# Last expert layer of a 1-core megakernel: half of the routed tiles turned by DMA, POOL's work in two parts per group, late gathers in the weights' place

## Chip, cores and metric

One core of one Trainium2 chip. The metric is the device time of one launch in microseconds. Before the change three runs gave 1920.95, 1926.91 and 1927.06 us; the median is 1926.91 us.

## What is computed

Two layers, each a residual attention and a residual expert feed-forward, on 16 sequences of 256 tokens with 256 features:

```python
x = x + tanh(g_xattn[0]) * xattn0(layernorm(x), ctx)
x = x + tanh(g_ffn[0])   * moe0(layernorm(x))
x = x + tanh(g_xattn[1]) * xattn1(layernorm(x), ctx)
x = x + tanh(g_ffn[1])   * moe1(layernorm(x))      # the part that is changed

def moe1(x):                    # 4096 tokens, 16 experts of width 128, 4 per token
    tidx, tw = route(x)         # sigmoid scores, best 2 of 4 groups, best 4 experts
    h  = silu(x @ gate_w[e].T) * (x @ up_w[e].T)          # per chosen expert
    routed = sum_k tw[k] * (h @ down_w[e_k].T)
    shared = (silu(x @ sh_gate.T) * (x @ sh_up.T)) @ sh_down.T   # width 256
    return routed + shared
```

## The kernel before

The kernel is written as hand-ordered streams, one per engine, in blocks that end with a barrier. Fp32 values are carried as two fp16 halves, upper and lower, so that a product is three matmuls.

The last layer (`moe1`) takes the tokens in four blocks of 1024. Each token row (two halves, 512 fp16) is **scattered** by POOL with indirect DMAs into a DRAM table `routed` of its block, ordered by expert. A table has 48 tiles of 128 rows, taken as 12 **groups** of 4 tiles, so there are 48 groups (r = 0 to 47). For a group, SP loads its 4 tiles into one of three buffers in `r_space` (L764, 512 KB). PE turns them, two tiles at a time (8 transposes into one PSUM bank, `turn_rows`, L1984), and ACT copies each half out to `m_rowsT` (`take_rows`, L2162, 128x1024). PE then makes the hidden layer (`routed_hidden`, L2040, 12 matmuls a half), ACT and DVE make silu, the product (L2169, L2266) and its two halves (L2176, L2272), PE turns these (`turn`, L2053), DVE copies them out (L2278), PE makes the down product (`routed_down`, L2014), ACT copies that to `m_y` (`evict`, L2188) and SP stores it to DRAM (L1875, 512 KB). POOL **gathers** the four expert rows of each token back (L1918) and DVE adds them with their weights to `x_res` (`combine`, L2287, 8 instructions for a pair of token tiles). Eight **shared jobs** of 512 tokens go through the shared expert, two ahead of the groups and six behind (L1999, L2014, L2297).

What one step r of the loop over groups does:

- PE: turn half 0 of group r+1, hidden half 0 of r, down of r-2, turn half 1 of r+1, hidden half 1 of r, load the experts' numbers of r+1 into registers, turn the hidden layer of r-1.
- ACT: silu(r-1), take half 0 of r+1, upper half of the hidden layer, take half 1 of r+1, evict(r-2). A take waits for the hidden matmuls two places back, since `m_rowsT` has two buffers; evict(r) waits for the store of r-3, since `m_y` has three.
- DVE: hiddenT copy (r-2), product and lower half (r-1), in some steps a piece of the routing of a later block, and `combine` of a pair in the steps of `PAIR_AT` (20, then every second step from 30 to 48).
- SP: load(r) once the buffer's rows have been turned, then store(r-6).
- POOL: behind the hidden matmuls of r-1, four scatters or gathers (`PACED`, `PER_GROUP = 4`). A gather waits for `used`: it has four token tiles of buffer (`GB = 4`).

The last pairs of token tiles (11 to 15) are combined among the shared jobs behind the groups, by `COMBINE_BEHIND`; SP's `finish(b)` stores block b of the output, 1 MB each.

## Time and profile before

| | |
|---|---|
| median of three runs | 1926.91 us (1920.95 to 1927.06) |
| profiled execution | 1910.97 us, its span 1908.7 us |
| granted TensorE clock, mean | 0.945 |
| PE busy | 1651.9 us, 87% |
| DVE / ACT / POOL busy | 62% / 53% / 40% |
| DMA | 256.99 MB, 135 GB/s over the span |

Columns of a window row: stretch, length, then busy time with instruction counts for each engine, the granted clock of TensorE (1.0 is full speed), the share of time that a DMA engine was busy, and GB/s. In a timeline row the first number is the start in us from the span's start, the second the length, and the bracket gives the idle time before it and what ended it. "Remote" or "unknown" there means that the profile has no releaser. The last layer runs from about 1450 us to the end.

### The profile page before, as it was taken

The page shows a single profiled execution, that of the slowest core. Times are in us where ns is not written, and L with a number is a line of the kernel's source. Part 1 is how long each engine was busy: PE and PEld are TensorE (multiplying, and loading weights), DVE is VectorE, ACT ScalarE, POOL GpSimd, SP SyncE. Part 2 cuts the span into 40 slices and gives each one's busy share as a digit, 9 for nine tenths or more (in the row PEclk, how much of TensorE's full clock was granted, in tenths as well). Part 3 has the DMA queues.
Part 4 walks back from the last instruction along what each step waited for, and adds up shares of the span by engine and source line. Part 5 has one row for each costly group of instructions (what it writes and reads, how often), then busy time and mean ns, then how long its engine had stood idle before and what let it go on. Part 6 is the DMA issues. An engine that isn't in the chain of part 4 may idle for free. (4 is left out here: it accounts for less than half of the span.)

```text
span 1908.7 us, 44330 instructions
## 1 busy us (share of the span) xinstructions
PE 1651.9 (87%) x16920; PEld 1256.1 (66%) x16920; DVE 1188.1 (62%) x2667; ACT 1005.9 (53%) x1744; POOL 763.4 (40%) x932
## 2 busy tenths in 40 slices
PE   4699999758999999999995899999886898888885
PEld 3355666437888888888883566665643777776753
DVE  4678887735555565565566788777762556345546
ACT  4377877635445444444433456645544576555541
POOL 2155657875310101000036334423651535565534
PEclk9699999978999999999997999989997999999898
DMA  9753333214645544544224434423243456677523
GB/s 288 208 117 68 72 60 68 57 41 133 203 150 196 172 139 167 195 158 135 67 84 107 99 80 79 71 55 58 76 125 144 164 200 233 232 235 250 190 90 121
DMA packets 297700, 256.99 MB, mean 135 GB/s; under 512 B 198047, under 2 KB 270155, under 8 KB 296216
## 3 DMA queue, kind: packets, MB, share of 16 engines
q1 hardware_dynamic: 271256, 168.84, 32.5%
q0 software_dynamic: 26240, 85.32, 13.4%
q8 instruction: 141, 2.31, 0.5%
q14 instruction: 63, 0.52, 0.1%
HBM read 102.98 MB, written 107.74 MB: 110 GB/s over the span
## 5 line engine op out<-in xcount | busy, mean ns | idle before, releaser
L1643 PE MATMUL ps<-m_xT,m_w_halves 128*128 128x256 f16 x3360 | 413.9, 273 | 2.2 <-issue 2.2
L1643 PEld LDWEIGHTS ps<-m_xT,m_w_halves 128*128 128x128 f16 x3360 | 329.4, 98 | 41.4 <-issue 2.8
L1158 ACT ACTIVATE a_probs<-ps 128x1024 f32<-128x1024 f32 (+1 forms) x256 | 234.8, 917 | 183.8 <-PE ps L995 181.9
L1662 PE MATMUL ps<-m_w_halves,m_hiddenT 128*128 128x256 f16 x1680 | 229.8, 273 | 5.1 <-DVE m_hiddenT L1758 4.6
L1274 POOL TENSOR_TENSOR a_probs<-a_probs,a_half_above 128x512 f32<-128x512 f32 x128 | 162.3, 1270 | 157.2 <-ACT a_probs L1158 156.6
L1719 ACT ACTIVATE m_hiddenT<-m_hidden 128x256 f16<-128x256 f32 x280 | 116.6, 416 | 197.6 <-DVE m_hidden L1755 191.6
L1758 DVE TENSOR_TENSOR m_hiddenT<-m_hidden,m_hiddenT 128x256 f16<-128x256 f32 x280 | 119.2, 426 | 135.1 <-ACT m_hiddenT L1719 130.7
L1610 POOL DMA_DIRECT2D expert_out<-m_y x40 | 28.9, 722 | 434.8 <-DVE m_y L1738 432.2
L2162 ACT ACTIVATE m_rowsT<-ps 128x1024 f16<-128x1024 f16 x112 | 115.9, 1035 | 154.0 <-remote 93.8
L1357 DVE TENSOR_REDUCE a_qT<-ps 128x4 f16<-128x1024 f32 x128 | 156.5, 1223 | 51.1 <-PE ps L1006 50.2
L1662 PEld LDWEIGHTS ps<-m_w_halves,m_hiddenT 128*128 128x128 f16 x1680 | 163.5, 98 | 26.9 <-DVE m_hiddenT L1758 7.2
L995 PE MATMUL ps<-a_Q,a_K 32*128 32x256 f16 (+1 forms) x2048 | 145.6, 261 | 34.2 <-DVE a_qT L1357 25.0
L1918 POOL DMA_INDIRECT m_gathered<-routed_out,r_routed_row x128 | 127.6, 997 | 113.4 <-DVE x_res L2287 46.6
L1755 DVE TENSOR_TENSOR m_hidden<-ps,m_silu 128x256 f32<-128x256 f32 x280 | 117.9, 421 | 81.9 <-ACT m_silu L1715 77.9
L1715 ACT ACTIVATE m_silu<-ps 128x256 f32<-128x256 f32 x280 | 105.6, 377 | 102.3 <-PE ps L1643 99.1
L1354 DVE TENSOR_REDUCE a_block_max<-ps 128x6 f32<-128x768 f32 x128 | 121.7, 951 | 60.4 <-PE ps L1006 58.8
L995 PEld LDWEIGHTS ps<-a_Q,a_K 32*128 32x128 f16 x2048 | 81.8, 93 | 114.2 <-issue 80.4
L2040 PE MATMUL ps<-m_w_halves,m_rowsT 128*128 x1152 | 149.0, 279 | 2.7 <-issue 2.6
L748 POOL DMA_INDIRECT routed<-r_halves,r_routed_row x96 | 96.6, 1007 | 132.1 <-issue 38.3
L1026 PE MATMUL ps<-a_probs,a_v_ext 128*32 128x256 f32 (+1 forms) x2048 | 126.6, 366 | 1.8 <-POOL a_probs L1274 1.8
L2040 PEld LDWEIGHTS ps<-m_w_halves,m_rowsT 128*128 128x128 f16 x1152 | 108.0, 100 | 21.7 <-issue 5.6
L1006 PE MATMUL ps<-a_K,a_Q 32*128 32x256 f16 (+1 forms) x1024 | 96.3, 267 | 10.3 <-DMA a_K<-a_kT 5.5
(319 smaller groups left out, 3070.3 us busy)
## 6 DMA issues: line engine op xcount, KB each, us to landing
routed<-m_zeros POOLq DMA_DIRECT2D x32, 768.0 KB
r_space<-routed SPq DMA_DIRECT2D x48, 512.0 KB
routed_out<-m_y SPq DMA_DIRECT2D x48, 512.0 KB
r_w_load<-in_L_w SPq DMA_DIRECT2D x24, 896.0 KB
dispatched<-r_xT SPq DMA_DIRECT2D x10, 1024.0 KB, 6.6
expert_out<-m_y POOLq DMA_DIRECT2D x40, 256.0 KB
a_ctx_in<-in_ctx SPq DMA_DIRECT2D x32, 256.0 KB
m_experts_load<-in_L_experts SPq DMA_DIRECT2D x18, 384.0 KB, 3.5
```

The source lines that it names most:

```text
L995: last = mm(SC[:, b_, c0:c0 + S - q0], lhs[r, g, kt * P:(kt + 1) * P], rhs[r, g, q0:S], start=not second and not causal_band, stop=second ...
L1026: last = mm(psum[j * SLOT:(j + 1) * SLOT, 6, (g % 2) * S + q0:(g % 2 + 1) * S], v[:, i % 4, kt, g * GH + j, :], pr[:, g % 2, j, kt * S:(kt ...
L1158: A(pr[:, g % 2, 2 * jp:2 * jp + 2, :], SC[:, :, 0:SPAN], ACT.Exp, scale=1.0 / math.sqrt(DH)).then_inc(asem["ex"], 1)
L1274: pool.tensor_tensor(two, two, half[:, :].unsqueeze(1).unsqueeze(1).broadcast_to([P, 2, 2, P]), ALU.mult).then_inc(asem["mask"], 1)
L1354: last = V.tensor_reduce(bmax[:, h0:h0 + 2, :], MX[:, :, 0:SPAN].rearrange("p h (b k) -> p h b k", k=P), AX.X, ALU.max, negate=True)
L1357: last = V.tensor_reduce(qT2[:, m % 3, :, h0:h0 + 2, DH].rearrange("p t h -> p h t"), MX.rearrange("p h (t k) -> p h t k", t=TT), AX.X, AL ...
L1643: last = mm(psum[:, v % HB, m * CH:(m + 1) * CH], wh[:, u, ws_, m, d_ * F0 + f_ * P:d_ * F0 + (f_ + 1) * P], xT[:, q % XB, xs_ * KT + d_, ...
L1662: last = mm(psum[:, 4 + 2 * (q % 2) + t, 0:D], hT[:, hs_, f_, t * P:(t + 1) * P], wh[:, u, ws_, 2, f_ * D:(f_ + 1) * D], start=f_ == 0 and ...
L1755: V.tensor_tensor(hp[:, v % 2, :], psum[:, v % HB, CH:2 * CH], hsb[:, v % 2, :], ALU.mult)\
L1758: V.tensor_tensor(hT[:, 1, v % FT, :], hp[:, v % 2, :], hT[:, 0, v % FT, :], ALU.subtract)\
L1918: pool.indirect_dma_start(yb[:, nt % GB, k, :], None, eo[b], bass.IndirectOffsetOnAxis(ap=rows[:, nt, k:k + 1], axis=0)).then_inc(got[nt % ...
L2040: last = mm(psum[:, 2 * (q % 2) + half, t % 2 * 2 * P:(t % 2 + 1) * 2 * P], xd[:, l % 2, xs_ * KT + d_, t * P:(t + 1) * P], both, start=k ...
```

## The change

- The first two tiles of each group are no longer loaded and turned by PE. `turn_routed_rows` brings them by two transposing DMAs from `routed` straight into the turned layout, in `r_space`, whose three places now hold turned rows (they take the part of `m_rowsT`, also for the shared jobs). The last two tiles are loaded into a new buffer `m_routed_rows` and turned by PE and taken by ACT as before. So `turn_rows(.., 0)` and `take_rows(.., 0)` do nothing for a routed group.
- SP issues, for group r: the load of two tiles; then, behind a wait for the hidden matmuls of group r-3, the two transposing DMAs; then store(r-6).
- PE's turn of half 1 waits for all three transfers of its group.
- POOL's four scatters or gathers of a step are split: two behind the hidden matmuls, two behind the first half of the down matmuls of r-2.
- The gathers of the last block (token tiles 24 to 31) go into the place of the routed experts' weights. Those of tiles 28 to 31 have semaphores of their own and wait for no `combine`.
- `COMBINE_BEHIND` takes pairs 11 to 15 behind jobs 1 to 5, so pair 15 is combined ahead of the last job's add. The last block's output is stored in three parts (512, 256 and 256 KB).

ACT's stream in a step of the groups' loop, before (names as in the profile; the brackets are semaphores waited for; `m1_rows_turned` is PE's turn, `f_h_done` the hidden matmuls):

```order
L2169 ACTIVATE m_silu<-ps 128x512 [waits f_gated,f_h_done]
L2162 ACTIVATE m_rowsT<-ps 128x4x256 [waits f_h_done,m1_rows_turned]
L2176 ACTIVATE m_hidden_halves<-m_hidden 128x512 [waits m1_hidden_turned,f_gated]
L2162 ACTIVATE m_rowsT<-ps 128x4x256 [waits f_h_done,m1_rows_turned]
L2188 ACTIVATE m_y<-ps 128x512 [waits m1_y_sent1,m1_y_done]
L2188 ACTIVATE m_y<-ps 128x512 [waits m1_y_done]
```

and with the change:

```order
L2214 ACTIVATE m_silu<-ps 128x512 [waits f_gated,f_h_done]
L2221 ACTIVATE m_hidden_halves<-m_hidden 128x512 [waits m1_hidden_turned,f_gated]
L2207 ACTIVATE r_space<-ps 128x4x256 [waits f_h_done,m1_rows_turned]
L2233 ACTIVATE m_y<-ps 128x512 [waits m1_y_sent1,m1_y_done]
L2233 ACTIVATE m_y<-ps 128x512 [waits m1_y_done]
```

The take of half 0 is gone, and the one that is left stands behind the upper half.

SP's stream about the store of the first output block, before (`m1_y_out` is ACT's evict, `m1_combined` DVE's combine):

```order
L764 DMA r_space<-routed 128x4x512 [waits m1_rows_turned]
L1875 DMA routed_out<-m_y 128x4x256 [waits m1_y_out]
L1881 DMA out_x<-x_res 128x8x256 [waits m1_y_out,m1_combined]
L764 DMA r_space<-routed 128x4x512 [waits m1_rows_turned]
L1875 DMA routed_out<-m_y 128x4x256 [waits m1_y_out]
```

and with the change:

```order
L1902 DMA routed_out<-m_y 128x4x256 [waits m1_y_out]
L1908 DMA out_x<-x_res 128x8x256 [waits m1_y_out,m1_combined]
L1892 DMA m_routed_rows<-routed 128x2x512 [waits m1_rows_turned]
L765 DMA_TRANSPOSE r_space<-routed 128x4x128 [waits f_h_done]
L765 DMA_TRANSPOSE r_space<-routed 128x4x128
L1902 DMA routed_out<-m_y 128x4x256 [waits m1_y_out]
```

A store now stands behind a wait for hidden matmuls and two transposing DMAs.

The diff, cut to its core:

```diff
@@ helpers
+    def turned_rows(place):
+        return r1["space"][:, place % XB1 * ROWS_T:(place % XB1 + 1) * ROWS_T].rearrange("p (a n) -> p a n", a=2 * KT)
...
+    def turn_routed_rows(sp, place, r):
+        for t in range(2):
+            r0 = (r % GROUPS1 * QT + t) * P
+            sp.dma_start_transpose(turned_rows(place)[:, :, t * P:(t + 1) * P], routed[r // GROUPS1][r0:r0 + P, :])\
+              .then_inc(x_in[r % XB1], 16)
@@ end of attention(1), sync
-                    for r in range(XB1):
-                        load_routed_rows(sp, r)
+                    turn_routed_rows(sp, 2, 0)
@@ moe1
-        xd = sb("rowsT", [P, 2, 2 * KT, CH], F16)
+        xr = sb("routed_rows", [P, XB, 2, 2 * D], F16)
+        late_rows = wh.rearrange("p s e n -> p (s e n)")[:, 0:RT * K1 * D * 2].bitcast(F32)\
+            .rearrange("p (t k d) -> p t k d", t=RT, k=K1)
+        LATE = (RG - 1) * RT
+        def rows_gathered(nt):
+            if nt >= LATE + GB:
+                return got_late[nt - LATE - GB], 16 * K1
+            return got[nt % GB], GOT0 + 16 * K1 * (nt // GB + 1)
-        COMBINE_BEHIND = {1: 11, 3: 12, 4: 13, 5: 14}
+        COMBINE_BEHIND = {1: 11, 2: 12, 3: 13, 4: 14, 5: 15}
+        def turned_until(l):
+            return l + min(l, L0) + max(l - L1, 0)
@@ moe1, sync
                 def load(r):
-                    sp.wait_ge(xp_done, 2 * (L0 + r - XB + 1))
+                    l = L0 + r
+                    if r >= XB:
+                        sp.wait_ge(xp_done, turned_until(l - XB) + 1)
...
+                    r0 = (r % GROUPS * QT + 2) * P
+                    sp.dma_start(xr[:, r % XB, :, :], ...).then_inc(x_in[r % XB], 16)
+                    if r:
+                        sp.wait_ge(h_done, H0 + last_unit(l - XB) + 1)
+                        turn_routed_rows(sp, l, r)
...
-                for b in range(1, RG):
+                for b in range(1, RG - 1):
                     finish(b)
+                for pairs, job, half in ((2, 6, 1), (4, 7, 0), (4, 7, 1)):
+                    sp.wait_ge(used, RT * K1 * (RG - 1) + 2 * K1 * pairs)
+                    sp.wait_ge(y_out, 2 * place_of_job(job) + half + 1)
...
@@ moe1, gpsimd
-                        if nt >= GB and k == 0:
+                        if GB <= nt < LATE + GB and k == 0:
                             pool.wait_ge(used, 2 * K1 * ((nt - GB) // 2 + 1))
...
                 for r in range(NR):
                     pool.wait_ge(h_done, H0 + U0 + r)
+                    paced(r, 0)
+                    if r >= 2:
+                        pool.wait_ge(y_done, 2 * (L0 + r - 2) + 1)
+                    else:
+                        pool.wait_ge(xp_done, 2 * (L0 + r + 2))
+                    paced(r, 1)
@@ moe1, tensor: turn_rows, routed_hidden
                         if half == 0:
-                            pe.wait_ge(x_in[r % XB], X0[r % XB] + 16 * (r // XB + 1))
-                        tile = [rows_of(r)[:, t, :] for t in range(QT)]
+                            return
+                        pe.wait_ge(x_in[r % XB], X0[r % XB] + 48 * (r // XB + 1))
+                        tile = [None, None] + [xr[:, r % XB, t, :] for t in range(2)]
...
-                    pe.wait_ge(xp_out, 2 * l + half + 1)
                     if half == 0:
+                        pe.wait_ge(x_in[r % XB], X0[r % XB] + 48 * (r // XB + 1))
                         pe.wait_ge(g_done, H0 + q - 1)
+                    else:
+                        pe.wait_ge(xp_out, turned_until(l + 1))
@@ moe1, scalar: take_rows
-                    if l >= L1 + JB:
+                    routed_place = L0 <= l < L1
+                    if l >= L1 + JB or routed_place and half == 0:
                         return
...
-                    if l >= 2:
-                        act.wait_ge(h_done, H0 + last_unit(l - 2) + 1)
+                    if l >= XB:
+                        act.wait_ge(h_done, H0 + last_unit(l - XB) + 1)
@@ moe1, vector, end
                 add_job(JA + JB - 1)
-                combine(15)
```

## Rows read from the trace of the kernel before

**Rows 1.** Windows: groups r = 0 to 8, 8 to 31 and 31 to 47.

```profile
1493.53:1551.28 57.75, 51.77 (x537) 45.34 (x537) 31.97 (x91) 38.17 (x60) 22.52 (x22) 0.94 0.55 186
1551.28:1707.30 156.02, 133.31 (x1439) 113.78 (x1436) 73.61 (x157) 96.32 (x146) 91.48 (x92) 1.00 0.70 233
1707.30:1825.05 117.75, 94.94 (x930) 77.98 (x928) 59.04 (x110) 62.98 (x96) 63.89 (x65) 0.93 0.65 209
```

**Rows 2.** Chain of waits, 1676 to 1690 us: start us, us, what.

```profile
1681.73 1.03 ACT m_rowsT L2162
...
1682.90 0.61 PE ps L1984 x8
...
1686.13 1.84 PE ps L1984 x8
...
1687.99 1.03 ACT m_rowsT L2162
```

**Rows 3.** Timeline, PE, the same group.

```profile
1683.35 1.47 PE L2040 MATMUL ps<-m_w_halves,m_rowsT 128*128 x12
...
1684.66 1.47 PE L2014 MATMUL ps<-m_w_halves,m_hiddenT 128*128 x12
...
1685.97 0.61 PE L1984 MATMUL ps<-ident,r_space 128*128 128x128 f16 x8
...
1686.41 1.47 PE L2040 MATMUL ps<-m_w_halves,m_rowsT 128*128 x12
...
1687.72 0.61 PE L2053 MATMUL ps<-ident,m_hidden_halves 128*128 128x128 f16 x8
```

**Rows 4.** Timeline, ACT, DVE and POOL, the same group.

```profile
1677.09 0.94 POOL L1918 DMA_INDIRECT m_gathered<-routed_out,r_routed_row  x1 [0.30 <-issue]
...
1682.65 1.08 ACT L2188 ACTIVATE m_y<-ps 128x512 f32<-128x512 f32 x2
...
1683.61 0.62 ACT L2169 ACTIVATE m_silu<-ps 128x512 f32<-128x512 f32 x1
...
1684.99 0.66 ACT L2176 ACTIVATE m_hidden_halves<-m_hidden 128x512 f16<-128x512 f32 x1
...
1685.68 0.69 DVE L2272 TENSOR_TENSOR m_hidden_halves<-m_hidden,m_hidden_halves 128x512 f16<-128x512 f32 x1 [0.74 <-issue]
```

**Rows 5.** Groups of instructions, 1551.28 to 1707.30 us: busy us, mean ns | idle before.

```profile
L2162 ACT ACTIVATE m_rowsT<-ps 128x1024 f16<-128x1024 f16 x46 | 47.8, 1039 | 51.6 <-remote 34.1 <-PE ps L1984 17.4
```

**Rows 6.** DMA queues, 1551.28 to 1707.30 us: packets, MB, share of 16 engines.

```profile
q1 hardware_dynamic: 24288, 24.12, 46.3%
q0 software_dynamic: 4365, 11.93, 22.9%
```

**Rows 7.** Timeline: SP in the first expert layer.

```profile
738.11 2.52 SPq L1560 DMA_TRANSPOSE m_xT<-dispatched  x2
```

**Rows 8.** DMA queues, 738 to 742 us: mean share in tenths, 40 slices of 0.1 us.

```profile
DMA  9779196990000037999741000001489996300006
```

**Rows 9.** DMA in the last attention, 1140 to 1240 us.

```profile
DMA packets 19920, 7.28 MB, mean 73 GB/s; under 512 B 18443, under 2 KB 19491, under 8 KB 19907
...
q1 hardware_dynamic: 19283, 5.38, 33.3%
```

**Rows 10.** Page: mean DMA share in 40 slices of the span, tenths.

```profile
DMA  9753333214645544544224434423243456677523
```

**Rows 11.** Timeline: the last group's store, and the gather that waits for it.

```profile
1832.49 0.36 SPq L1875 DMA_DIRECT2D routed_out<-m_y  x1
...
1838.09 0.95 POOL L1918 DMA_INDIRECT m_gathered<-routed_out,r_routed_row  x1 [17.48 <-DMA routed_out<-m_y]
```

**Rows 12.** Timeline: POOL and DVE in the tail.

```profile
1855.69 0.94 POOL L1918 DMA_INDIRECT m_gathered<-routed_out,r_routed_row  x1 [7.67 <-DVE x_res L2287]
...
1895.38 0.95 POOL L1918 DMA_INDIRECT m_gathered<-routed_out,r_routed_row  x1 [0.30 <-issue]
...
1900.17 3.63 DVE L2287 SCALAR_TENSOR_TENSOR x_res<-m_gathered,r_gather_weight,x_res 128x256 f32<-128x256 f32 x8
```

More of the change, by code:

```diff
@@ L1825, in moe1 @@
         stored = sem("stored")
+        got_late = [sem(f"m1_got_late{u}") for u in range(NT - LATE - GB)]
+        def rows_gathered(nt):
+            if nt >= LATE + GB:
+                return got_late[nt - LATE - GB], 16 * K1
+            return got[nt % GB], GOT0 + 16 * K1 * (nt // GB + 1)
         H0 = CHUNKS0 * FT0
@@ L1883, in _ @@
                 LAG = XB + 3
+                load(0)
                 for c in range(4):
                     sp.dma_start(wh[:, :, c * 4:(c + 1) * 4, :], w16[:, :, c * 4:(c + 1) * 4, :]).then_inc(w_in[1], 16)
-                for r in range(XB, NR + LAG):
+                for r in range(1, NR + LAG):
                     if r < NR:
@@ L1892, in _ @@
                         finish(0)
-                for b in range(1, RG):
+                for b in range(1, RG - 1):
                     finish(b)
-                sp.wait_ge(stored, 16 * RG)
+                for pairs, job, half in ((2, 6, 1), (4, 7, 0), (4, 7, 1)):
+                    sp.wait_ge(used, RT * K1 * (RG - 1) + 2 * K1 * pairs)
+                    sp.wait_ge(y_out, 2 * place_of_job(job) + half + 1)
+                    t0, t1 = (LATE, LATE + QT) if job == 6 else (LATE + QT + 2 * half, LATE + QT + 2 * half + 2)
+                    sp.dma_start(out_dram[:, t0:t1, :], x[:, t0:t1, :]).then_inc(stored, 16)
+                sp.wait_ge(stored, 16 * (RG + 2))
             @block.gpsimd
@@ L1924, in _, with paced @@
                 OPS = RT * K1
-                for r in range(NR):
-                    pool.wait_ge(h_done, H0 + U0 + r)
+                def paced(r, part):
                     for what, b, begin, first, end in PACED:
@@ L1930, in _ @@
                             what_of = scatter if what == "scatter" else gather
-                            what_of(b, j, min(j + PER_GROUP, end))
+                            what_of(b, j + part * PER_GROUP // 2, min(j + (part + 1) * PER_GROUP // 2, end))
+                for r in range(NR):
+                    pool.wait_ge(h_done, H0 + U0 + r)
+                    paced(r, 0)
[4 more added lines that the diff above has]
+                    paced(r, 1)
                 gather(2, 28, OPS)
@@ L1999, in shared_hidden @@
                                 last = mm(psum[:, 2 * i + m, :], ws[:, ws_, i, w0:w0 + P],
[L2000 removed]
+                                          turned_rows(l)[:, xs_ * KT + d_, :], start=k == 0, stop=k == 5)
                                 k += 1
```

31 lines of the change are left out of this document (14 added, 17 removed).

## The prediction

> **What bounds the kernel now.** I read the windows first. The groups' loop of the last layer makes 23 groups in 156.02 us, 6.78 us each, and then 16 in 117.75 us, 7.36 us each; the first eight take 7.22 us each [rows 1]. PE is busy 133.31 of the 156.02 us, so it is near its limit but not at it, and a DMA engine is busy 0.70 of the time.
>
> The chain of waits says what closes the loop. It runs from a take (ACT, 1.03 us) to PE's turn (0.61), the hidden and down matmuls, PE again from 1686.13 to 1687.97, and the next take at 1687.99: one turn of the loop is 6.26 us [rows 2]. PE's turn of half 0 stands behind the take of half 1, because both use one PSUM bank, so a turn and a take lie in series with everything else PE does. PE's own starts show what it needs without that turn: hidden half 0 1683.35 to 1684.66, 1.31 us; down 1.31; turn of half 1 0.44; hidden half 1 1.31; turn of the hidden layer 0.45 (the 0.61 less its overlap, as for the other turn): **4.82 us** [rows 3]. One oddity counts below: the turn of half 1 is over at 1686.58, yet ACT takes it only at 1687.99 [rows 2, 3]. 46 takes idled 51.6 us in all, 34.1 of them with no releaser named [rows 5]. I take that delay as it is.
>
> Behind the groups the tail is bound by POOL and DVE in turns: POOL waited 7.67 us for a combine at 1855.69, and the last eight adds of DVE end at 1903.80, 4.9 us ahead of the span's end [rows 12].
>
> **The change, part by part.** The sum is made against the profiled execution's 1910.97 us (span 1908.7 plus 2.3 around it), which lies 16 us under the median; I carry the difference over to the median.
>
> *PE and ACT in a group.* Gone per group: 8 transposes (about 0.45 us of PE) and one take (47.8/46 = 1.04 us of ACT) [rows 3, 5]. More than that, the take of half 1 is now wanted only by the next group's turn and second hidden half, some 3 us later, so it leaves the loop. What is left is the chain through ACT and DVE: with hidden matmuls done at 0, take 0.3 to 1.3, evict 1.08, silu 0.62, product 0.7, upper 0.66, lower 0.69: about 5.1 us, before PE may turn the hidden layer [rows 4]. PE turns it one group later, at 4.82 plus, so two groups take at least 5.1 + 0.45 + 4.37 = 9.9 us: **5.0 us a group**.
>
> *POOL.* Four indirect DMAs a group at 0.94 + 0.30 = 1.24 us are 5.0 us [rows 4]. The split puts two behind the hidden matmuls and two behind the down matmuls some 2.7 us later, when the first two are just over. With a wake-up or two of 0.3 to 0.5 us it needs **5.3 to 5.5 us**. It did not bind at 6.78. What is queued behind its new wait are only its own later gathers, and DVE's combine waits for those.
>
> *SP.* Per group one load and one store at 0.36 us [rows 11] and two transposing issues, 2.52 us [rows 7]: 3.2 us, under any group's time. The transposes of group r go out when the hidden matmuls of r-3 are done; PE wants them at its turn in step r-1, that is 2 x 5 - 1.75 = 8.3 us later. They need 0.3 + 2.5 for issue, and the second one's data ended about 0.8 us behind its issue [rows 7, 8]. Even with 2 to 3 us for the signal they are in time; I cost them at nothing. If that cover is gone, PE waits for them directly.
>
> *The DMA engines.* 0.70 of 6.78 us is 4.75 us of all 16 engines a group. Of that the plain queue has 0.463 x 6.78 = 3.14 us for 1 MB [rows 1, 6], so half a load, which goes, is 0.79. For a transpose there are two prices. In the first expert layer, from DRAM like here, two stand as two humps whose tenths add up to 49 each in slices of 0.1 us: 0.5 us each, 0.53 with rounding [rows 8]. In attention, from SBUF, 33.3 us went to 18443 packets of 256 bytes, that is 36 transposes of 512 packets with a few plain loads: at most 0.92 us each [rows 9]. So a group needs 4.75 - 0.79 + 1.06 = 5.0 us or, at the upper price, 5.8. The fullest slice of the page shows nine tenths [rows 10]; divided by 0.9 these are **5.6 and 6.4 us**. I take 5.6 as nearest, since the source is DRAM in both.
>
> A rule of the Trainium skill lies between: Advanced Engine Details and Errata, section X-Bar Transpose (TRN2), says that transposing DMAs are as fast as plain ones. By it two would cost 0.79 us and a group 4.75/0.9 = 5.3 us; the humps say about a third more, and the humps are what I use.
>
> *The sum over the groups.* 5.6 is the largest bound; bursts of SP's and POOL's transfers will not mesh, so I take 5.8 where no combine runs: 23 x (6.78 - 5.8) = **22 us**. In the last 16 groups DVE has a combine of 3.63 us every second step [rows 12]. It starts behind the lower half at about 5.1 and holds up the hiddenT copy until 9.4 us; the down matmuls want that at 5.8 + 1.75 = 7.5. So PE stalls about 1.9 us in two steps, nearly 1 us a group, where at 6.26 us it just fitted: 5.8 + 1.0 = 6.8, and 16 x (7.36 - 6.8) = **9 us**. The first eight, with routing pieces on all engines, go from 7.22 to 6.6: **5 us**. The first group's rows come by DMA and two turns less stand ahead of it: **1 us**.
>
> *The tail.* The gathers of tiles 24 and 25 go out as before, those of 26 and 27 still wait for combine 11 (POOL 1855.69). Then 16 more follow with no wait: the last starts at 1855.69 + 23 x 1.27 = 1884.9, where it was 1895.38, so 10.5 us sooner [rows 12]. DVE reaches the last combine then, because pairs 12 to 15 stand one job earlier. The last output part is 256 KB, not 1 MB: up to 2 us less of transfer at 3.14 us a MB, of which I count 0.5. Tail **11 us**. The gathers into the weights' place collide with nothing: they wait for the last group's stores as before.
>
> Sum: 22 + 9 + 5 + 1 + 11 = 48 us. 1910.97 - 48 = 1863, and from the median 1926.9 - 48 = **1879 us**. Late next is POOL and the DMA engines together.
>
> **The rivals.**
>
> *The DMA engines bind* at the upper price: 6.4 us a group. For it: 49,000 more small packets, and a stage at 0.70 already [rows 1, 9]. Against: the humps [rows 8]. The gain is 23 x 0.38 + 16 x 0.25 + 3 + 1 + 11 = 28 us: 1899.
>
> *PE and the ACT-DVE chain alone bind*, 5.1 us: the engines mesh well. 23 x 1.68 + 16 x 1.15 + 7 + 1 + 11 = 76 us: 1851. For it: PE's 4.82 us, with the granted clock at 1.00 in the 23 groups [rows 1, 3]; against: POOL's 5.3 to 5.5.
>
> *Only the tail gains.* If the late signal of the turn has a cause that also holds up the hidden layer's turn, the loop keeps its 6.3 to 6.8 us. 11 us from the tail and 1: 1915; within 0.3% if the tail gives half.
>
> *Slower: the stores come late.* Store(r) was issued one group ahead of what it now is: it stands behind the wait for the hidden matmuls of r and the two transposes, so it goes out 0.3 + 2.5 + 0.4 = 3.2 us behind them. Alone, the last store took 5.6 us from its issue to the waiting gather's start [rows 11], so 8.8 us, and ACT wants the buffer for evict(r) at 2 x 5.8 + 1.3 = 12.9. It decides once a store takes over 9.7 us. At 11 us two groups take 3.2 + 11 + 1.1 = 15.3, so 7.7 each, and ACT stands in front of silu: 23 x 0.9 + 16 x 0.3 = 26 us lost, 11 won: 1942. For it: one queue and 0.9 full engines; against: a margin of 4 us.
>
> *Slower: the transposing DMAs pass tile by tile.* At the 1.26 us that one of two issues took [rows 7], for each 128x128 tile, eight tiles a group would be 10.1 us, and 48 x (10.1 - 7) = 149 us lost: 2065. The humps speak against it, since four tiles pass in half a us [rows 8]. The rule of the Trainium skill behind it: VectorE: DVE Perf Modes, sections The three transpose paths and Rules for kernel authors, prices a 128x128 transpose at 390 ns on TensorE and 1309 ns by DMA, and advises TensorE where a PSUM destination will do. By that the change is a loss; the trace has four such tiles per 1.26 us of issue.
>
> **How the numbers follow.** Chances: the forecast 0.54, DMA-bound 0.20, well meshed 0.10, tail alone 0.09 (a third of it within 0.3%), late stores 0.06, tile by tile 0.01. Some 0.3%, 6 us, is what a measurement tells from no change. Faster 0.54 + 0.20 + 0.10 + 0.06 = 0.90, same 0.03, slower 0.07. The forecast's own width is 1865 to 1892 (5.5 to 6.1 us a group). The range reaches to the well-meshed case and over the DMA-bound one to short of the tail alone: 1853 to 1911.
>
> **What would show it.** Right: 48 takes fewer; groups without a combine at 5.6 to 6.1 us with a DMA share near 0.85; POOL nearly without idle time; the last gather some 40 us behind the first late one, less the wait for pair 11; DVE's copies of hiddenT late in every second step of the last 16 groups. Wrong: PE waiting for transfers of rows, or ACT's evict waiting for a store (late stores); DMA share at 0.9 with groups of 6.4 us (DMA-bound); groups still at 6.3 us or more with a free DMA (the turn's signal).

## The result and the profile after

The changed kernel is slower: 1932.01 us median (1918.81 to 1941.87) against 1923.4 us of the kernel before measured beside it, ratio 1.0043, 95% interval 1.0028 to 1.0058. The forecast was 1879 us. The profiled execution of the changed kernel is at its median (span 1930.1 us), that of before lies 12 us under its own, so the two profiles differ by more than the medians: 21.4 us of span. Windows of the changed kernel, cut at the same places as [rows 1] (PE's turn of the hidden layer of groups 0, 8, 31 and 47):

```profile
1493.05:1563.80 70.75, 53.36 (x474) 42.91 (x473) 32.57 (x91) 32.75 (x54) 24.55 (x26) 0.83 0.60 151
1563.80:1721.43 157.63, 128.84 (x1255) 104.67 (x1253) 72.70 (x156) 77.00 (x122) 94.04 (x93) 0.97 0.86 230
1721.43:1835.15 113.72, 83.44 (x816) 66.81 (x817) 59.33 (x111) 52.08 (x82) 61.54 (x64) 0.98 0.82 226
```

Against [rows 1] the first eight groups lost 13.0 us, the 23 lost 1.6, the last sixteen won 4.0. From there to the end of the span it is 95.0 us where it was 83.7, 11.3 lost; the start won 0.5. The sum is the 21.4. Two more profiles of the same program, on other chips (`e1_after_again` and `g1_after_on_another_chip` below), have 70.5 and 69.7 us for the first eight groups, 154.9 and 162.2 us for the 23, and 94.9 and 97.3 us behind the groups. So the losses at the start and at the end come back each time, and the 1.6 us of the 23 groups are no difference.

ACT's takes, PE and DVE in the 23 groups:

```profile
L2207 ACT ACTIVATE r_space<-ps 128x1024 f16<-128x1024 f16 x22 | 22.5, 1024 | 57.8 <-remote 46.2 <-PE ps L2026 10.5 <-issue 1.1
...
L2323 DVE COPY m_hiddenT<-ps 128x1024 f16<-128x1024 f16 x23 | 15.9, 691 | 48.1 <-PE ps L2097 30.6 <-remote 15.0 <-issue 2.2
...
L2056 PE MATMUL ps<-m_w_halves,m_hiddenT 128*128 x276 | 36.5, 284 | 11.6 <-DVE m_hiddenT L2323 5.0 <-issue 4.7 <-ACT m_y L2233 1.8
...
L2097 PE MATMUL ps<-ident,m_hidden_halves 128*128 128x128 f16 x185 | 14.3, 218 | 6.1 <-issue 6.1
```

Half of the takes are gone, as forecast, but the idle time that has no releaser did not go with them: 46.2 us on 22 takes, where it was 34.1 on 46 [rows 5], and PE has "issue" gaps that it hardly had.

The loss of the first eight groups is in one group. PE there:

```profile
1519.95 2.37 PE L2056 MATMUL ps<-m_w_halves,m_hiddenT 128*128 x10
1523.36 0.27 PE L2056 MATMUL ps<-m_w_halves,m_hiddenT 128*128 x1 [1.04 <-issue]
1524.77 0.27 PE L2056 MATMUL ps<-m_w_halves,m_hiddenT 128*128 x1 [1.15 <-issue]
...
1536.79 0.39 PE L2084 MATMUL ps<-m_w_halves,r_space 128*128 x1 [0.34 <-issue]
1537.50 1.89 PE L2084 MATMUL ps<-m_w_halves,r_space 128*128 x8 [0.33 <-issue]
```

ACT's timeline at the same time:

```profile
1537.58 0.29 ACT L743 ACTIVATE r_positions<-ps 128x144 f32<-128x144 f32 x1 [17.15 <-remote]
```

and POOL's, ahead of it and beside it:

```profile
1502.66 0.98 POOL L748 DMA_INDIRECT routed<-r_halves,r_routed_row  x1 [22.99 <-PE ps L2026]
...
1514.72 0.97 POOL L748 DMA_INDIRECT routed<-r_halves,r_routed_row  x1 [7.24 <-PE ps L2026]
1516.00 0.98 POOL L748 DMA_INDIRECT routed<-r_halves,r_routed_row  x1 [0.30 <-issue]
...
1533.92 0.98 POOL L748 DMA_INDIRECT routed<-r_halves,r_routed_row  x1 [0.30 <-issue]
```

POOL first waited 22.99 and 7.24 us for PE's turns (the kernel before has one wait there, 7.33 us at 1490.07), then made up for it with 16 indirect DMAs in a row, one every 1.28 us. Some 8 us into them PE falls to single matmuls, many with 1.0 to 1.2 us ahead that nothing in the profile explains, and ACT takes positions that PE had finished at 1520 only at 1537.58. The same picture stands behind the groups, PE first:

```profile
1876.21 0.28 PE L2026 MATMUL ps<-ident,m_x_halves 128*128 128x128 f16 x2
1876.97 0.33 PE L2026 MATMUL ps<-ident,m_x_halves 128*128 128x128 f16 x3 [0.48 <-issue]
...
1889.80 0.59 PE L2041 MATMUL ps<-r_space 128*128 128x512 f16 x1 [0.42 <-issue]
1902.23 1.03 PE L2026 MATMUL ps<-ident,m_x_halves 128*128 128x128 f16 x8 [11.84 <-ACT r_space L2207]
```

POOL's timeline there:

```profile
1866.98 0.95 POOL L1951 DMA_INDIRECT m_w_halves<-routed_out,r_routed_row  x1 [8.03 <-DVE x_res L2332]
...
1896.09 0.95 POOL L1951 DMA_INDIRECT m_w_halves<-routed_out,r_routed_row  x1 [0.30 <-issue]
```

and ACT's:

```profile
1901.15 1.02 ACT L2207 ACTIVATE r_space<-ps 128x1024 f16<-128x1024 f16 x1 [27.85 <-remote]
```

POOL issues 24 gathers without a pause from 1866.98. PE stumbles 9.2 us into them, ACT stands 27.85 us, and both go on 4 to 5 us behind the end of the last gather. Nothing was won by it: the last gather is issued at 1896.09, where it was 1895.38 [rows 12].

### The profile page after: what moved, and what is told of

It reads as the page before. It is cut to its first block and busy times, and to the rows that moved or that the text cites. A ratio compares the mean times of both kernels' runs of the same rounds, so it can differ in the third digit from the quotient of the medians.

```text
span 1930.1 us, 43566 instructions
## 1 busy us (share of the span) xinstructions
PE 1641.4 (85%) x16536; PEld 1233.2 (64%) x16536; DVE 1188.4 (62%) x2667; ACT 966.5 (50%) x1696; POOL 761.7 (39%) x932
## 5 line engine op out<-in xcount | busy, mean ns | idle before, releaser
L1357 DVE TENSOR_REDUCE a_qT<-ps 128x4 f16<-128x1024 f32 x128 | 156.6, 1223 | 51.7 <-PE ps L1006 50.8
L2084 PE MATMUL ps<-m_w_halves,r_space 128*128 x1152 | 150.7, 279 | 14.1 <-issue 13.9
L2207 ACT ACTIVATE r_space<-ps 128x1024 f16<-128x1024 f16 x64 | 65.6, 1024 | 176.5 <-remote 123.3
L2084 PEld LDWEIGHTS ps<-m_w_halves,r_space 128*128 128x128 f16 x1152 | 109.0, 100 | 33.8 <-issue 19.1
L1951 POOL DMA_INDIRECT m_gathered<-routed_out,r_routed_row x96 | 93.7, 976 | 68.0 <-DVE x_res L2332 20.1
L2056 PE MATMUL ps<-m_w_halves,m_hiddenT 128*128 x576 | 78.1, 287 | 33.5 <-DVE m_hiddenT L2323 16.8
```

What stands on the lines that cost most here:

```text
L1357: last = V.tensor_reduce(qT2[:, m % 3, :, h0:h0 + 2, DH].rearrange("p t h -> p h t"), MX.rearrange("p h (t k) -> p h t k", t=TT), AX.X, AL ...
L2056: last = mm(psum[:, 6 + half, (t % 2) * D:(t % 2 + 1) * D], hT[:, u, hs_, t * P:(t + 1) * P], w2, start=k == 0, stop=k == total - 1)
L2084: last = mm(psum[:, 2 * (q % 2) + half, t % 2 * 2 * P:(t % 2 + 1) * 2 * P], turned_rows(l)[:, xs_ * KT + d_, t * P:(t + 1) * P], both, sta ...
```

## The experiments

Three theories are weighed. **A:** a long unbroken run of indirect DMAs on POOL holds up the other engines' instructions and signals. **B:** instructions are fetched late behind full DMA engines. **C:** the transposing DMAs are the cost. All ratios are to the kernel before on the same chip. The runs fell on chips of two kinds: on some the kernel before takes 1911 to 1926 us, as in the result, on two it takes 1837 to 1838 us. I call them the slower and the faster kind; at which of them a run was made is said each time.

**The kernel again (slower kind, before 1912).**

> The changed kernel, unaltered, in one more profile. Theory A (while POOL issues indirect DMAs without a pause, PE gets its instructions late): the three stretches in which PE makes single matmuls with idle time that nothing explains return at the same places, behind the 17 DMAs in a row near 1515 us and the 24 in a row near 1867 us: first eight groups 70 us, groups to end 94 us, ratio 1.004 to before. Theory B (PE's instructions are fetched late behind full DMA engines): stalls return too, but at places where the DMA share is high, not near 1525 us where it was low. Theory C (chance): the stalls lie elsewhere or are absent in this profile, and the parts' lengths move by over 10 us.

Ratio 1.0092 (1.0059 to 1.0125). Both stops are back at their places, with 70.45 us for the first eight groups. Chance is out: the stops belong to the program. The end behind the groups takes 94.9 us.

**POOL's first waits in the right unit.** In steps 0 and 1 POOL waits for the count of turns of rows. The change counts one such turn per routed group where it was two, but left the wait's numbers:

```diff
-                        pool.wait_ge(xp_done, 2 * (L0 + r + 2))
+                        pool.wait_ge(xp_done, turned_until(L0 + r + 2))
```

> POOL's waits of steps 0 and 1 count turned rows by the new count (6 and 7 in place of 8 and 10), so POOL is not held for 23 and 7 us and has nothing to catch up with. Theory A: the 17 DMAs in a row go, and with them the 24 us of group 3; the first eight groups take 52 to 58 us in place of 70.8, and the whole is 12 to 18 us faster than the changed kernel: ratio 0.995 to 0.998 to before. Theory B: the transfers and so the fetches stay, the stall stays in part: 0 to 5 us. Theory C: no difference.

Same chip: 1.0031 (1.0016 to 1.0046), 0.6% or 11 us faster than the run above. Group 3 takes 7.43 us, the first eight 58.8.

**POOL unsplit.**

```diff
                     paced(r, 0)
-                    if r >= 2:
-                        pool.wait_ge(y_done, 2 * (L0 + r - 2) + 1)
-                    else:
-                        pool.wait_ge(xp_done, 2 * (L0 + r + 2))
                     paced(r, 1)
```

> The changed kernel with POOL's four indirect DMAs of a step in one piece behind the hidden matmuls, as before, and without its second wait. Theory A: no catch-up at the start, so the first eight groups return to 52 to 58 us; but runs of four make POOL late more often, and the loop of groups 8 to 31 stays at 6.8 us or gets 0.1 us longer: 10 to 17 us faster than the changed kernel, ratio about 0.997. Rival (the split itself is what the shorter loop needs, by POOL's 5.3 us): 23 groups take 0.3 us more each, +7 us, against the start's gain: ratio 1.000.

Same chip: 1.0018 (1.0001 to 1.0034); first eight 58.8 us, the 23 155.8. What the split cost was its stale wait; the second wait itself wins nothing that can be told. It also did not do what the change says: in the 23 groups of the run above, POOL's second part often followed its first at once, and of 29 unbroken runs 17 still had four DMAs. So the two runs do not compare runs of two with runs of four. Two windows of this kernel behind the groups, while POOL issues 24 gathers in a row from 1850.66:

```profile
1860.00:1870.00 10.00, 3.52 (x15) 1.01 (x12) 1.00 (x2) 0.00 (x0) 7.56 (x9) 0.86 0.39 118
1870.00:1883.00 13.00, 0.00 (x0) 0.00 (x0) 0.00 (x0) 0.00 (x0) 8.29 (x9) 0.50 0.34 101
```

For 13 us PE, DVE and ACT do nothing at all, with the DMA engines busy for a third of the time. In the first stop of the changed kernel, 1524 to 1537 us, their share is 0.28. The instruction queues moved one packet at 1855 us and the next at 1885.5, when ACT had already gone on at 1884.58. That speaks against B.

**The old tail.** Gathers of the last block through the four buffers again, the old `COMBINE_BEHIND`, the last output in one piece.

```diff
-        LATE = (RG - 1) * RT
+        LATE = NT
-        COMBINE_BEHIND = {1: 11, 2: 12, 3: 13, 4: 14, 5: 15}
+        COMBINE_BEHIND = {1: 11, 3: 12, 4: 13, 5: 14}
```

> The changed kernel with the tail of before: gathers of the last block through the four buffers, behind the combines, combine 15 last, the last 1 MB stored at once. Theory A: the 24 DMAs in a row behind the groups go and with them PE's stall of some 14 us there; the end behind the groups takes 84 us as before in place of 95: 8 to 12 us faster than the changed kernel. Rival (the late gathers as such pay, as forecast, 11 us, and the stall has another cause): 3 to 11 us slower than the changed kernel.

Same chip: 1.0031 (1.0014 to 1.0049), with the first stop still in it (70.45 us). Behind the groups it takes 85.5 us. So the new tail cost some 0.6%, as much as the stale wait.

**The tail alone, on the kernel before.**

> The kernel before with nothing but the new tail (late gathers into the weights' place, pairs 12 to 15 one job earlier, the last output in three parts). Theory A (an unbroken run of indirect DMAs on POOL holds up the signals and instructions of the other engines, and more the longer it is): behind the groups stand 24 gathers in a row, PE and ACT stop some 9 us into them and go on when the last one is issued; the end behind the groups takes 92 to 100 us in place of 83.7, and the whole is 5 to 12 us slower than before, ratio 1.003 to 1.006. Rival (the forecast's tail): 5 to 11 us faster, 0.994 to 0.997.

This fell on the faster kind (before 1838): 0.9959 (0.9934 to 0.9984), a gain, against theory A. Its repeat there:

> The same kernel as e5_tail_only. Theory A2: where before takes 1900 us or more, the 24 gathers in a row behind the groups stop PE and ACT some 9 us into the run, the end behind the groups takes 90 to 95 us in place of 84, ratio 1.003 to 1.006; where before takes 1840 us, 0.996 again. Rival (the late gathers gain on every chip, and the stall of the changed kernel needs the transposes too): 0.994 to 0.997.

0.9982 (0.9961 to 1.0003), no difference that can be told. And on the slower kind (before 1926):

> The same kernel as e5_tail_only. Where before takes 1900 us or more: theory A (long runs hold up the signals) 1.003 to 1.006, the end behind the groups 90 to 95 us in place of 84; rival (the stop needs the transposes) 0.994 to 0.997. Where before takes 1838 us: 0.996 to 0.998 as twice before, which tells nothing new.

1.0019 (0.9992 to 1.0045): the whole time does not show a loss, the end behind the groups does (94.7 us for 83.7). One kernel, two behaviours. PE of the tail alone behind the groups on the slower kind:

```profile
1874.11 0.22 PE L2004 MATMUL ps<-ident,m_x_halves 128*128 128x128 f16 x1
1875.48 0.22 PE L2004 MATMUL ps<-ident,m_x_halves 128*128 128x128 f16 x1 [1.15 <-issue]
...
1894.52 0.58 PE L2019 MATMUL ps<-m_rowsT,r_space 128*128 128x512 f16 x1 [0.79 <-issue]
```

and on the faster kind:

```profile
1804.27 0.61 PE L2004 MATMUL ps<-ident,m_x_halves 128*128 128x128 f16 x8
1805.98 2.75 PE L2019 MATMUL ps<-m_rowsT,r_space 128*128 128x512 f16 x12 [1.10 <-ACT m_rowsT L2182]
1808.56 0.61 PE L2004 MATMUL ps<-ident,m_x_halves 128*128 128x128 f16 x8
1809.01 2.75 PE L2019 MATMUL ps<-m_rowsT,r_space 128*128 128x512 f16 x12
1811.60 2.78 PE L2034 MATMUL ps<-r_space,m_hiddenT 128*128 128x256 f16 x24
```

though POOL's 24 gathers ran there from 1795.42 to 1825.48 with the same 0.30 us between them. The end behind the groups takes 94.7 and 70.3 us. The stop needs no transposes, and it came on no chip of the faster kind.

**Pauses between the gathers.** On the unsplit kernel with the new tail:

```diff
+                        if nt >= LATE and k % 2 == 1:
+                            pauses.append(0)
+                            pool.memset(xr[:, 0, :, :], 0.0).then_inc(paused, 1)
+                            pool.wait_ge(paused, len(pauses))
```

> The changed kernel unsplit, with a memset of 128x1024 fp16 behind every second gather of the last block, and the next gather behind that memset, so that POOL has no run of more than two. Each pause is 1 to 2 us, sixteen of them lengthen POOL's work by 16 to 32 us. Theory A: PE and ACT show no gap above 5 us behind the groups, though POOL's last gather comes later; the end takes no longer than in the unsplit kernel without pauses, 92 us, or is up to 8 us shorter. Rival (transfers into the weights' place hinder PE, or all gathers hinder it alike, in runs or not): PE's gap of 19 us stays or grows by the pauses, the end takes 100 us or more.

> The same kernel as e8_paused_gathers. Theory A2: where before takes 1900 us or more, ACT's gap of 28 us goes, none above 5 us stays behind the groups, and the end behind the groups takes 80 to 88 us in place of the unsplit kernel's 92: ratio 0.995 to 1.001. Rival (any gathers hinder PE, in runs or not): the gap grows by the pauses, the end takes 100 us or more, ratio above 1.004.

Both fell on the faster kind: 1.0062 (1.0038 to 1.0087) and 1.0075 (1.0049 to 1.0101), which says nothing of stops, since there are none there. On the slower kind:

> The same kernel as e8_paused_gathers. Where before takes 1900 us or more: theory A no gap of PE above 5 us behind the groups, the end 80 to 88 us; rival (gathers hinder PE in runs or not) a gap of 19 us and more, the end 100 us. Where before takes 1838 us: 1.006 to 1.008 as twice before.

**0.9918** (0.9900 to 0.9936), while the changed kernel itself on that chip has 1.0041:

> The changed kernel, unaltered. If the late signals belong to some chips only: where before takes about 1838 us, group 3 still costs POOL its stale waits, but PE runs on through the 17 DMAs in a row and groups 2 to 5 take under 35 us in all; behind the groups PE has no gap of 12 us, and the end takes 70 us as with the new tail alone; ratio 1.003 to 1.008 from the transposes. Where before takes 1900 us or more: group 3 at 18 us or more, the end at 95 to 105 us, ratio 1.004 to 1.010. Rival (a run this long stops the engines on every chip): a gap of over 10 us in group 3 on a fast chip too.

(1.0012 to 1.0070; group 3 22.6 us, the end 97.3 us.) By the profiles 12 us of the difference lie in the first eight groups, since the unsplit kernel has no stale wait, and 17 us in the end. PE with pauses, in the stretch where it stopped without them:

```profile
1866.18 0.61 PE L2027 MATMUL ps<-ident,m_x_halves 128*128 128x128 f16 x8
1867.87 2.75 PE L2042 MATMUL ps<-r_space 128*128 128x512 f16 x12 [1.08 <-DVE m_hidden L2312]
1870.46 0.61 PE L2027 MATMUL ps<-ident,m_x_halves 128*128 128x128 f16 x8
1870.90 2.75 PE L2042 MATMUL ps<-r_space 128*128 128x512 f16 x12
1873.49 2.78 PE L2057 MATMUL ps<-r_space,m_hiddenT 128*128 128x256 f16 x24
```

and POOL's part of it:

```profile
1868.15 0.95 POOL L1952 DMA_INDIRECT m_w_halves<-routed_out,r_routed_row  x1 [0.27 <-POOL m_routed_rows L1957]
1869.41 0.95 POOL L1952 DMA_INDIRECT m_w_halves<-routed_out,r_routed_row  x1 [0.31 <-issue]
1870.36 0.97 POOL L1957 MEMSET m_routed_rows<- 128x1024 f16 x1
```

All 32 gathers still go out, to the same place, 3.45 us for two where it was 2.5. PE has no gap from issue, ACT's takes have none without a releaser, and the end takes 80.4 us. One PE gap is above the 5 us of theory A, 8.92 us at 1894.66, and it has a plain cause: PE waits for DVE, and DVE for the late gathers. A pause of 1 us behind every second gather made the end 14 us shorter than the tail alone had it on the same chip. The transfers that stand ahead of the stop are not its cause by themselves: SP's store of 1 MB fills the DMA engines to 0.92 from 1872 to 1876 us in the changed kernel, to 0.93 from 1861 to 1865 us here, and to 0.88 on the faster kind, the last two without a stop. Theory A holds for the tail; whether the run's length or its rate counts is not told apart, since the pause changes both.

**The late gathers on SP's queue.** The last 16 gathers are replaced by plain DMAs of fixed rows, so that the last four token tiles add up other rows.

> The changed kernel unsplit, with the 16 gathers of the last four token tiles replaced by 16 plain DMAs of the same size to the same place on SP's queue, from fixed rows (so the last tiles' sums are of other rows). Theory A: POOL has 16 gathers left, in two runs of eight; ACT's gap of 28 us goes, gaps of 3 to 6 us at the end of each run stay, and the end behind the groups takes 60 to 75 us in place of 92: 17 to 30 us faster than the unsplit kernel. Rival (the transfers into the weights' place or the memory traffic are the cause, whoever issues them): PE and ACT stop as before while the 16 arrive, and the end stays above 85 us.

It fell on the faster kind: 0.9972 (0.9946 to 0.9998), the end 68.9 us. Without a stop to remove it decides nothing.

**The transposes alone** (unsplit, old tail).

> The changed kernel with POOL unsplit and the old tail, so that the transposing DMAs and what belongs to them are alone. Theory A: both losses are gone; groups in 112 to 114 us for the last sixteen and 155 to 157 for the 23 before, first eight 58 to 59, the end 84 us: 1905 to 1909 us on the scale where before is 1912, ratio 0.996 to 0.998. Rival (transposes cost as much as they save, and the parts above were only shifted): ratio 0.999 to 1.001.

> The same kernel as e6_transposes_alone, on another chip where it can be had. Chips differ: in the first four runs the kernel before took 1912 us, in the last four 1838 us, with ACT's takes on time there and DMA engines at 0.84 to 1.05 in the groups' loop. Theory A2 (on the slower chips POOL's runs of indirect DMAs hold up signals, on the faster one they do not, and there the transposes fill the DMA engines): where before takes 1900 us or more, the shorter loop outweighs, ratio 0.994 to 0.998; where it takes 1840 us, 1.007 again. Rival (transposes cost more than they save on every chip): 1.003 to 1.008 here too.

Both on the faster kind: 1.0073 (1.0047 to 1.0100) and 1.0090 (1.0055 to 1.0125). The window of the 23 groups, with transposes (the first of the two runs):

```profile
1535.66:1669.10 133.44, 122.16 (x1254) 103.26 (x1252) 72.50 (x158) 78.08 (x125) 92.52 (x91) 0.99 1.05 267
```

and without, in the kernel with the split alone (below):

```profile
1543.28:1676.90 133.62, 130.53 (x1438) 118.28 (x1436) 73.39 (x157) 96.85 (x147) 90.45 (x92) 0.97 0.84 272
```

There PE is the bound before (130.5 of 133.6 us), and the DMA share goes from 0.84 to 1.05. PE's 8.4 us are won and nothing comes of them. The first profile is the fastest of its 12 executions; the second, near its median, has 137.6 us. The loop of the kernel before without the split, in the two profiles of the tail alone, has 131.4 and 131.5 us. So the transposes cost 2 to 6 us in the 23 groups, and in the last sixteen (91.0 and 97.3 us against 87.1 to 87.3) 4 to 10.

**Plain DMAs in place of transposing ones**, same bytes and places in pieces of 512 bytes; those tiles are not turned, so their products are of other numbers.

```diff
-            sp.dma_start_transpose(turned_rows(place)[:, :, t * P:(t + 1) * P], routed[r // GROUPS1][r0:r0 + P, :])\
+            sp.dma_start(turned_rows(place)[:, 2 * t:2 * t + 2, 0:2 * P],
+                         routed[r // GROUPS1][r0:r0 + P, :].rearrange("p (a n) -> p a n", a=2))\
```

> The kernel with the transposes alone (POOL unsplit, old tail), with each transposing DMA replaced by a plain one of the same 128 KB from the same rows to the same places in pieces of 512 bytes (so those tiles are not turned, and the results of their tokens are of wrong numbers). Theory C (the transposing DMAs take 0.8 to 1.05 us of all DMA engines each, twice a plain one's 0.4): where before takes 1838 us, the DMA share in groups 8 to 31 falls from 1.05 to 0.85 to 0.9, a group takes 5.1 to 5.3 us in place of 5.8, and the ratio goes from 1.008 to 0.985 to 0.993. Rival (the added waits and the order on SP's queue cost it): groups stay at 5.8 us, ratio 1.005 to 1.009.

On the slower kind: 0.9916 (0.9895 to 0.9937), the same as the paused kernel beside it, which has its transposes, but also another tail. Against that kernel's profile the DMA share fell from 0.82 to 0.69 and the 23 groups still took 160.2 us against 159.1 (the profile is the slowest of six executions, 7.5 us above their median). So nothing shows that the DMA engines bind this loop on the slower kind. That the transposes cost nothing there is not shown either: their own kernel was not run on it, and the old tail's 1.0031 less the 0.6% of the stale wait puts it at about 0.997 by estimate, above the 0.9916 of the plain DMAs.

**The split alone, on the kernel before.**

> The kernel before with nothing but POOL's work in two parts of two a step. Theory A2: where before takes 1900 us or more, runs of two end before the signals are late, the take no longer waits 1.4 us for a turn that is over, and groups 8 to 31 take 5.8 to 6.3 us in place of 6.8: 10 to 20 us faster, ratio 0.990 to 0.995; where before takes 1840 us, within 3 us of it. Rival (the split only shifts POOL's work): no difference on either.

On the faster kind: 1.0009 (0.9989 to 1.0029), as expected for it. ACT's takes there:

```profile
L2170 ACT ACTIVATE m_rowsT<-ps 128x1024 f16<-128x1024 f16 x46 | 47.8, 1038 | 27.8 <-PE ps L1992 27.8
```

The tail alone has the loop of the kernel before, without the split, and on the faster kind its takes are as quiet:

```profile
L2182 ACT ACTIVATE m_rowsT<-ps 128x1024 f16<-128x1024 f16 x46 | 47.7, 1038 | 25.4 <-PE ps L2004 25.4
```

Against [rows 5] this is the difference of the two kinds: the 34.1 us without a releaser are 0, and the group takes 5.71 us (5.81 with the split) in place of 6.78. It is not slower transfers: the plain queue's packets took 46.3% of 156.02 us, 72 us, before, and 55.6% of 131.39 us, 73 us, here.

**Pauses in the loop too** (a memset of 128x64 behind every second indirect DMA), without and with the transposes, slower kind (before 1911).

> The kernel before with the new tail, a pause (memset of 128x1024, next gather behind it) behind every second late gather and a short pause (memset of 128x64) behind every second indirect DMA in the groups' loop. Theory A, where before takes 1900 us or more: signals are on time in the loop too, groups 8 to 31 take 5.3 to 5.9 us each in place of 6.8 (as on the faster chips), the end 80 us: 20 to 35 us faster than before, ratio 0.982 to 0.990. Rival (the slower loop has another cause, such as slower transfers): groups stay at 6.6 us or more, only the end gains 4 us, ratio 0.997 to 1.000. Where before takes 1838 us: POOL's work of 5.0 us a group grows to 5.6, the loop loses 5 to 10 us, 1.003 to 1.006.

> The changed kernel with POOL unsplit and the same pauses in the loop and behind it. Theory A, where before takes 1900 us or more: no stops in the loop; it is then bound by the DMA engines at 0.9 to 1.05 and POOL's 5.6 us, groups 8 to 31 take 5.8 to 6.1 us: ratio 0.984 to 0.991, and not below h1's, since the transposes' DMA time takes the place of PE's. Rival (transposes gain as forecast once the signals are on time): 5 us or more below h1. Second rival (another cause of the slow loop): 6.7 us a group, ratio 0.991 as with pauses behind the loop alone. Where before takes 1838 us: 1.006 to 1.010.

0.9960 (0.9941 to 0.9978) and 0.9938 (0.9914 to 0.9962). The 23 groups take 154.0 and 156.6 us, the ends 80.0 and 83.0. ACT's takes in the first:

```profile
L2193 ACT ACTIVATE m_rowsT<-ps 128x1024 f16<-128x1024 f16 x46 | 47.5, 1032 | 51.1 <-PE ps L2015 27.3 <-remote 23.8
```

A third of the idle time without a releaser is gone (23.8 for 34.1), and neither theory's number came for the 23 groups together. The trace tells why. All 23.8 us stand beside gathers and none beside scatters, while before 31.2 of the 34.1 us stood beside scatters. POOL beside scatters, then beside gathers:

```profile
1642.13 0.98 POOL L748 DMA_INDIRECT routed<-m_x_halves,r_routed_row  x1 [0.31 <-issue]
1644.04 0.97 POOL L748 DMA_INDIRECT routed<-m_x_halves,r_routed_row  x1 [0.78 <-POOL m_unread L1923]
...
1684.95 0.95 POOL L1947 DMA_INDIRECT m_gathered<-routed_out,r_routed_row  x1 [0.30 <-issue]
1686.34 1.20 POOL L1947 DMA_INDIRECT m_gathered<-routed_out,r_routed_row  x1 [0.27 <-POOL m_unread L1923]
```

and the take that follows the gathers:

```profile
1689.47 1.02 ACT L2193 ACTIVATE m_rowsT<-ps 128x1024 f16<-128x1024 f16 x1 [3.87 <-remote]
```

The same memset holds two scatters 0.93 us apart, from the end of one to the start of the next, and two gathers only 0.44 us. The seven groups 18 to 24, which have scatters alone, took 5.69 us each in place of 6.75, and 5.57 with the transposes; on the faster kind they take 5.36. The six groups behind them, most of them with gathers, took 7.74 in place of 6.46. So theory A's number came in the loop too, where the pause was long. Gathers are not immune to pauses: behind the groups they stand 1.24 us apart and hold up nothing. That in the loop it is the pause's length and not the kind of DMA is likely by this, not shown. With and without transposes the intervals overlap: they neither win nor lose here that can be told.

## Why the prediction was wrong

**The 23 groups, 22 us forecast, 1.6 lost.** The step that failed is the sentence on the oddity of [rows 2, 3], "I take that delay as it is". I removed what stood around the delay and left it at 1.4 us on a turn. It is no property of the take: on the faster kind it does not exist. It goes with POOL's runs. In the 23 groups of the kernel before ACT has 15 gaps above 0.5 us without a releaser, and 14 of them end 0.7 to 1.2 us behind the end of POOL's fourth DMA; the late take at 1687.99 comes 0.8 us behind it. Behind the groups it is 5.9 and 5.4 us (ACT in the profile of before, at 1846.60 and 1867.00) about the end of runs of eight, 6.1 us in the middle of a run of sixteen (1888.58), and 27.85 us beside the run of 24. With the take of half 0 gone, the time went to the take that was left (46.2 us on 22), to DVE's copy of hiddenT (remote 15.0 against 3.9) and to PE's own issue gaps. Groups of 5.4 us occur, but a group in which PE or a signal is held takes 7 to 11.

With that delay the bound was misread. PE needs 4.82 us without the turn of half 0 and 0.45 more with it, 5.27 us, and 5.27 us is what 13 of the 23 groups take on the faster kind with the turn still in (`f2_tail_only`). So of the 6.78 us that I put down to the turn and the take in series, 1.07 were held signals: without them the same loop takes 5.71 us on the faster kind. The forecast 5.8 us a group did come, 5.80 us with the transposes on the faster kind, but nothing was won by it there. Where the signals are on time on the slower kind (groups 18 to 24 with pauses), the transposes gain 0.12 us a group, where 0.98 were forecast.

**POOL, priced at 5.3 to 5.5 us of its own time.** Right as its time, wrong as its only effect. On the slower kind its runs are a cost to all others, and I read the new wait in the diff as harmless ("only its own later gathers" behind it). In steps 0 and 1 its unit was stale; the waits held POOL for 30 us where it had been 7, and the catch-up of 16 in a row cost group 3 its 16 us. That is the 13.0 lost where 5 were forecast as won, and it stood in the diff: one counter changed its meaning, one reader of it did not.

**The tail, 11 us forecast, 11.3 lost.** Its mechanism, 16 gathers that follow without a wait, is what happened, and the absence of waits is what hurt. On the faster kind it gained 6.1 us (70.2 for 76.3 us behind the groups), so there the working was right in sign and half its size.

**The last sixteen groups, 9 us forecast, 4.0 won.** The sign is right on the slower kind, in all three profiles (113.7, 111.6 and 114.4 us for 117.8); on the faster the transposes lose 4 to 10 us there. **The start** won 0.5 of 1 us.

**The DMA engines.** 5.0 us a group was forecast, with 0.53 for a transpose. Measured: 0.86 of 6.85 us is 5.9. The queue of the plain and the transposing DMAs has

```profile
q1 hardware_dynamic: 43235, 23.95, 58.0%
```

58.0% of 6.85 us is 3.97, where it was 3.14 [rows 6]; less 0.79 for half a load, that is 0.81 us for each transpose, near the upper price of [rows 9]. By the same sum the plain pieces of 512 bytes took 0.47 (47.2% of 6.97 us), and the transposes on that chip, in the paused kernel, 0.75 (55.6% of 6.92 us). The rule of the Trainium skill (Advanced Engine Details and Errata, section X-Bar Transpose (TRN2)) that transposing DMAs are as fast as plain ones does not hold in these runs: they took 1.6 to 1.7 times the plain ones' engine time. The limit of 0.9 that I divided by was no limit: the share reached 1.05. So the DMA-bound rival had the price right; what it forecast, a gain of 28 us, was still not there: on the slower kind the held signals bound the loop, and on the faster one the group was at 5.71 us before.

**The rivals.** "Only the tail gains" named the late signal as a possible cause that also hits the hidden layer's turn, at 0.09; of its two parts one came, the loop stayed at 6.85 us. The other did not, its tail lost. The stores never came late (ACT's evict has no wait for a store among its idle time), and tile by tile is out. No rival had a slower end through POOL. I had the trace for it: ACT's three gaps without a releaser beside the runs of eight and sixteen stand in the profile of before, in a tail that I read as bound "by POOL and DVE in turns" [rows 12], and I did not look at ACT there.

**What stays open:** what the held signals are in the chip, and why some chips have them; whether length or rate of the run decides, and why a run of sixteen let go in its middle; how long a pause must be, between the 0.44 us that did not help and the 0.93 us that did; what the transposes cost on the slower kind. The changed kernel itself, the plain DMAs and the pauses in the loop were not run on the faster kind, and the transposes alone, the split alone and the late gathers on SP's queue not on the slower. No version here is shown to beat the kernel before on both kinds: the unsplit kernel with pauses wins 0.8% on the slower and loses 0.6 to 0.8% on the faster; the new tail alone wins 0.2 to 0.4% on the faster (one of its two intervals reaches 1.0003) and nothing that can be told on the slower.

## What to carry to other kernels

An idle time that the profile can't explain is a term of the sum, not a background: find what it goes with (here, POOL's runs) before removing work beside it. Where a change makes a semaphore count in another unit, list every reader of it, the pacing waits too. Waits in a stream of indirect DMAs may be what keeps the other engines running; when such waits are removed, put pauses in their place, of about 1 us here, and try both, on more than one chip. Then look in the trace whether each pause is there: one memset gave 0.93 us in one place and 0.44 in another.

## What the runs showed of the hardware that I had not expected

- On chips where the kernel before takes 1911 to 1926 us, 7 to 9 us into an unbroken run of 16 or 24 indirect DMAs on POOL (one per 1.25 to 1.28 us) PE issues single matmuls, mostly 0.7 to 1.4 us apart, and ACT gets no signal for 17 to 28 us; a memset of 1 us behind every second one ended it. (A run of sixteen in the tail of before held ACT for 6.1 us only.) On two chips with 1837 to 1838 us a run of 24 did nothing. The DMA engines were at 0.28 to 0.41 meanwhile. The Trainium skill (SBUF — State Buffer, section Who interferes with whom) says that "DMA never contends with a compute engine"; these rows show engines held while DMAs are issued from POOL, in what they issue and are told, not in how long one of their instructions takes (ACT's take is 1.02 us in and out of the stops).
- On those chips a run of four costs too: 14 of 15 unexplained gaps of ACT in the groups' loop end 0.7 to 1.2 us behind the run's last DMA. With 0.93 us between pairs of scatters the gaps were gone and a group took 5.69 us in place of 6.75; with 0.44 us between pairs of gathers they stayed.
- The same program differs by 4 to 5% between chips. Of the 71 us between the profiles of before and of the tail alone on the faster kind, 55 lie in the 39 groups 8 to 46: 6.78 against 5.71 us a group in the first 23, at a granted clock of 1.00 in both.
- A transposing DMA of 128 KB took 0.75 to 0.81 us of the 16 engines on two chips of the slower kind by the sums above, and up to 0.87 on one of the faster (68.9% of 5.98 us is 4.12, less 2.38 for half a load and a store, in `f1_transposes_alone`), a plain one in 512-byte pieces 0.47.
